# Self-attention of a decoder layer: exponentials become the stationary operand, sums come as a column, results are turned by TensorE, and the steps stand in a new order

## What is computed

```
q = einsum('ntc,hdc->nhtd', x, w_q); k = ...w_k; v = ...w_v
a = einsum('nhtd,nhsd->nhts', q, k) / sqrt(dk)
a = where(t < s, -inf, a);  a = softmax(a, axis=-1)
y = einsum('nhts,nhsd->nthd', a, v).reshape(n, t, h*d)
return y @ w_o
x = x + attn(layernorm(x), ...)
```

## Time and profile before

| | us |
|---|---|
| median of 3 runs | 2052.72 |
| lowest and highest run | 2051.78, 2059.14 |
| span of the profiled execution | 2060.4 |
| startup of self-attention (to the fourth NM), in the profile | 0 to 134 |
| self-attention, steady, in the profile | 134 to 852 |
| its last units | 852 to 894 |
| the rest of the layer | 894 to 2060 |

### The profile page before, as it was taken

The page is one execution under the profiler, slowest core; times in us unless marked ns, Lnnn a source line. Parts: engine busy times, 40 slices in busy tenths (PEclk is TensorE's granted clock), DMA queues, the critical chain, the costliest instruction groups (busy, mean ns, idle before and its releaser), DMA issues. The chain is left out here.

```text
span 2060.4 us, 40889 instructions
## 1 busy us (share of the span) xinstructions
PE 1842.1 (89%) x13992; PEld 972.5 (47%) x13992; DVE 1385.2 (67%) x3320; ACT 1291.6 (63%) x2477; POOL 1098.1 (53%) x1102
## 2 busy tenths in 40 slices
PE   4899999999999999979999999977899999588885
PEld 2456666666666666633333233322334443345553
DVE  5576666666666656457778777865798888554457
ACT  2677777777667776647777777773666666234442
POOL 2466666666566665633434433223667777455554
PEclk8899999999999999989999999997999999799998
DMA  6223232222322222313333113301011100233355
GB/s 187 69 64 71 61 71 59 66 63 63 73 63 60 65 67 55 74 44 63 62 63 61 29 37 63 57 14 33 21 30 67 50 22 22 85 92 114 93 191 193
DMA packets 102523, 141.00 MB, mean 68 GB/s; under 512 B 16400, under 2 KB 66352, under 8 KB 102320
## 3 DMA queue, kind: packets, MB, share of 16 engines
q1 hardware_dynamic: 95408, 119.44, 24.7%
q0 software_dynamic: 6912, 18.95, 2.5%
HBM read 53.77 MB, written 33.90 MB: 43 GB/s over the span
## 5 line engine op out<-in xcount | busy, mean ns | idle before, releaser
L771 POOL TENSOR_TENSOR a_P_lo<-a_PR,a_P_hi 128x384 f16<-128x384 f32 (+1 forms) x384 | 379.2, 999 | 336.7 <-ACT a_P_hi L580 252.4
L1333 DVE TENSOR_REDUCE x_NM<-x_pm 128x1 f32<-128x512 f32 x512 | 342.1, 687 | 97.8 <-PE x_pm L1069 95.2
L1254 ACT ACTIVATE x_PR<-x_pS 128x512 f32<-128x512 f32 x512 | 300.7, 601 | 111.8 <-PE x_pS L1085 105.8
L700 DVE CUSTOM_DVE_ANT_0 a_pm<-a_pm,a_causal 128x128 f32<-128x128 f32 (+3 forms) x512 | 251.9, 497 | 145.2 <-PE a_pm L463 136.1
L577 ACT ACTIVATE a_PR<-a_pS 128x384 f32<-128x384 f32 (+1 forms) x384 | 202.4, 527 | 100.6 <-PE a_pS L486 85.5
L580 ACT ACTIVATE a_P_hi<-a_pS 128x384 f16<-128x384 f32 (+1 forms) x384 | 202.1, 526 | 44.5 <-PE a_pa L500 44.5
L710 DVE TENSOR_TENSOR a_Y<-a_pa,a_RS 64x512 f32<-64x512 f32 x128 | 88.0, 688 | 137.5 <-ACT a_RS L593 135.5
L463 PE MATMUL a_pm<-a_KA,a_QA 128*128 128x128 f16 (+3 forms) x512 | 149.2, 303 | 29.0 <-DVE a_NM L700 21.0
L1097 PE MATMUL x_pa<-x_PR,x_V 128*32 128x256 f32 x2048 | 168.0, 401 | 1.7
L484 PE MATMUL a_pS<-a_QA,a_KA 128*128 128x512 f16 (+3 forms) x512 | 153.0, 301 | 11.4 <-DMA a_QB<-a_NMT 5.6
L500 PE MATMUL a_pa<-a_P_hi,a_V_hi 128*128 128x512 f16 (+3 forms) x512 | 152.6, 301 | 3.6 <-POOL a_P_lo L771 3.2
(11 more groups left out here) (411 smaller groups left out, 4994.7 us busy)
## 6 DMA issues: line engine op xcount, KB each, us to landing
a_QA<-a_nat_q_hi SPq DMA_DIRECT2D x128, 128.0 KB, 2.3
first_keys<-sent SPq DMA_DIRECT2D x80, 129.0 KB
a_QB<-a_nat_q_lo SPq DMA_DIRECT2D x64, 128.0 KB, 2.4
a_KA<-a_nat_k_hi SPq DMA_DIRECT2D x64, 128.0 KB, 2.4
a_KA<-a_nat_k_lo SPq DMA_DIRECT2D x64, 128.0 KB, 2.4
a_KB<-a_nat_k_hi SPq DMA_DIRECT2D x64, 128.0 KB, 2.4
e_ga<-back SPq DMA_DIRECT2D x16, 512.0 KB
first_keys<-in_w SPq DMA_DIRECT2D x12, 512.0 KB
```

The lines of the kernel that those rows point to most:

```text
L700: eng.tensor_tensor_reduce(out=pm[i % 2][:, 0:n], in0=pm[i % 2][:, 0:n], in1=causal[:, T - n:T], scale=1.0, scalar=NEG, op0=ALU.add, op1=A ...
L771: eng.tensor_tensor(P16[1][:, m % RH, 0:n], PR[:, m % RF, 0:n], P16[0][:, m % RH, 0:n], ALU.subtract).then_inc(s_el, 1)
L1254: eng.activation(PR[:, kc, j, :], pS[i % 2][:, :], ACT.Exp, scale=SCALE).then_inc(s_e, 1)
L1333: eng.tensor_reduce(NM[:, v % 2, c:c + 1], ring_bank("max", v, n)[:, :], AX.X, ALU.max, negate=True).then_inc(s_red, 1)
```

## The change

- AV (L549 to L551 now): for each pair of a key block and a block of 128 queries, the block of exponentials is the stationary operand and V moves: 65 columns for the terms with `V_hi` (64 of V and a column of ones), 64 for `V_lo`. Ten pairs a head and three terms: 120 matmuls a unit in place of 48. Queries now lie on partitions, and the sum of each row is a column beside its 64 values.
- ACT no longer runs LN and EX. DVE takes the reciprocals of four sums a head (L746) and multiplies four blocks of 64 columns (L748).
- POOL writes high and low parts to `Y16`. PE turns them, 8 transposes of 128 columns for each pair of heads (YT, L495), into `pp[1]` (from u = 32 on into `pp[0]`), and DVE copies the bank to `YT` (L758). QK 3 and V 1 wait for these copies, since they use the same bank.
- V: one ACT pass and one DVE pass of 512 columns a half (DVE took two of 256). The presets of ones and zeros shrink to one memset.
- WO comes one unit later (u - 6), and the last units have order numbers of their own.
- All order numbers are new, with a turn of 25 in place of 27. This moves steps on all engines, SP's DMAs among them.

```diff
-    V = [sb(f"V_{n}", [P, 2, TT, GH, P], F16) for n in ("hi", "lo")]
+    VW, OW = 72, 68
+    V_hi = sb("V_hi", [P, 2, TT, GH, VW], F16)
+    V_lo = sb("V_lo", [P, 2, TT, GH, D], F16)
...
-    RS = sb("RS", [P, 2, T], F32)
-    Y = sb("Y", [P, 2, T], F32)
-    YT = [sb(f"YT_{n}", [P, 2, F // P, T], F16) for n in ("hi", "lo")]
+    RC = sb("RC", [P, 2, TT], F32)
+    Y = sb("Y", [P, 2, TT, P], F32)
+    Y16 = [sb(f"Y_{n}", [P, 2, TT, P], F16) for n in ("hi", "lo")]
+    YT = sb("YT", [P, 2, F // P, 2, T], F16)
...
-    TURN = 27.0
-        ("SP", "CK"): (19.104,),
-        ("SP", "NP"): (45.09,),
+SELF_TURN = 25.0
+    ("SP", "CK"): (13.946,),
+    ("SP", "NP"): (39.099,),
...
+            if c == 3:
+                after(eng, s_yo, 2 * u - 4)
...
+            if h == 1:
+                after(eng, s_yo, 2 * u - 3)
...
+        def turn_values(u, q):
+            eng.wait_ge(s_yh, q + 1)
+            eng.wait_ge(s_yl, q + 1)
+            if u < NU:
+                eng.wait_ge(s_lo, 4 * u + 2 + 2 * (1 - q % 2))
+            elif q % 2 == 1 and u < NU + 2:
+                eng.wait_ge(s_xr, u - 5)
+            else:
+                eng.wait_ge(s_yo, q)
+            for z in range(2):
+                for t in range(TT):
+                    o = (z * TT + t) * P
+                    m = eng.transpose(turned_bank(u)[:, :].bitcast(F16)[:, o:o + P], Y16[z][:, q % 2, t, :], k.id16[:, :])
+            m.then_inc(s_yt, 1)
...
-                    for n, (v, p) in enumerate(((0, 0), (1, 0), (0, 1))):
-                        m = eng.matmul(pa[j % 2][:, P * kc:T], V[v][:, u % 2, kc, j, :], P16[p][:, i % RH, a:a + T - P * kc],
-                                       start=(kc == 0 and n == 0), stop=(kc == TT - 1 and n == 2))
+                    for t in range(kc, TT):
+                        o = a + (t - kc) * P
+                        hi, lo = (z[:, i % RH, o:o + P] for z in P16)
+                        out = pa[j % 2][:, t * OW:t * OW + D + 1]
+                        eng.matmul(out, hi, V_hi[:, u % 2, kc, j, 0:D + 1], start=(kc == 0 and t == 0), stop=False, skip_group_check=True)
+                        eng.matmul(out[:, 0:D], hi, V_lo[:, u % 2, kc, j, :], start=False, stop=False, skip_group_check=True)
+                        m = eng.matmul(out, lo, V_hi[:, u % 2, kc, j, 0:D + 1], start=False, stop=(kc == t), skip_group_check=True)
...
-                    eng.activation(RS[outs, pair, :], pa[j % 2][sums, :], ACT.Ln).then_inc(s_ln, 1)
-                eng.activation(RS[:, pair, :], RS[:, pair, :], ACT.Exp, scale=-1.0).then_inc(s_rc, 1)
...
-                eng.tensor_tensor(Y[outs, pair, :], pa[j % 2][outs, :], RS[outs, pair, :], ALU.mult).then_inc(s_y, 1)
+                o = values_of(j)
+                eng.reciprocal(RC[:, j % 2, :], o[:, :, D]).then_inc(s_rc, 1)
+                eng.wait_ge(s_rc, GH * u + j + 1)
+                eng.tensor_tensor(Y[:, pair, :, j % 2 * D:(j % 2 + 1) * D], o[:, :, 0:D],
+                                  RC[:, j % 2, :].unsqueeze(2).to_broadcast([P, TT, D]), ALU.mult).then_inc(s_y, 1)
...
+                eng.tensor_copy(YT[:, b % 2, 2 * g + pair, :, :].rearrange("p z t -> p (z t)"),
+                                turned_bank(v)[:, :].bitcast(F16)).then_inc(s_yo, 1)
```

More of the change, by code:

```diff
@@ L323, in self_attention @@
-    FIRST = {"ST": -16, "RS": -13, "XN": -11, "XH": -7.5, "XL": -6}
-    TURNED = {"PE": (-1.6, -1.0), "DVE": (-1.2, -0.5)}
-    def at(engine, step, u, i=0):
-        return u * TURN + PLACE[engine, step][i]
+    def at(engine, step, u, i=0):
+        if step == "WO" and u >= NU:
+            return NU * SELF_TURN + SELF_END[step][u - NU] + (1 if engine == "DVE" else 0.1 * i)
+        if step == "YT" and u >= NU:
+            return NU * SELF_TURN + SELF_END[step][2 * (u - NU) + i] + (1 if engine == "DVE" else 0)
+        return u * SELF_TURN + SELF_PLACE[engine, step][i]
@@ L442, in projections @@
                     transpose_x(b, h)
-            for c in range(4 if u < NU else 0):
+            if NU <= u < NU + 2:
+                yield from project_out(u)
+            for c in range(2 if u < NU else 0):
                 yield at("PE", "QK", u, c)
                 project_qk(u, c)
+            if 0 <= 2 * u - 5 < 2 * NU:
+                yield at("PE", "YT", u, 0)
+                turn_values(u, 2 * u - 5)
+            for c in range(2, 4 if u < NU else 0):
+                yield at("PE", "QK", u, c)
+                project_qk(u, c)
+            if 0 <= 2 * u - 4 < 2 * NU:
+                yield at("PE", "YT", u, 1)
+                turn_values(u, 2 * u - 4)
             for h in range(2 if u < NU else 0):
@@ L706, in scale_values, with turned_out @@
                 yield at("DVE", "Y", u, j)
-                eng.wait_ge(s_rc, q + 1)
+                eng.wait_ge(s_av, US * u + NS * (j + 1))
                 after(eng, s_yl, q - 1)
-                outs, _ = rows_of(j)
-                eng.tensor_tensor(Y[outs, pair, :], pa[j % 2][outs, :], RS[outs, pair, :], ALU.mult).then_inc(s_y, 1)
+                o = values_of(j)
[3 more added lines that the diff above has]
+                                  RC[:, j % 2, :].unsqueeze(2).to_broadcast([P, TT, D]), ALU.mult).then_inc(s_y, 1)
+        def turned_out(u):
+            b, g = u // NG, u % NG
+            for pair in range(2):
+                q, v = 2 * u + pair, u + 2 + pair
+                yield at("DVE", "YT", v, 1 - pair)
+                eng.wait_ge(s_yt, q + 1)
+                after(eng, s_wo, NG * (b - 1))
+                eng.tensor_copy(YT[:, b % 2, 2 * g + pair, :, :].rearrange("p z t -> p (z t)"),
+                                turned_bank(v)[:, :].bitcast(F16)).then_inc(s_yo, 1)
         def split_weights():
@@ L739, in next_stage @@
                                              in1=nat[0][1 - half][:, n, :], op0=ALU.max, op1=ALU.subtract).then_inc(s_pl, 1)
[L741 to L746 removed]
+        eng.memset(V_hi[:, :, :, :, D:D + 1].rearrange("p b t j o -> p (b t j) o"), 1.0).then_inc(s_pre, 1)
+        side_by_side(over(scale_values), over(turned_out), over(reduce_max), over(projections, NU + 6), over(norm, B), split_weights(), next_stage())
     def gpsimd_program(eng):
```

169 lines of the change are left out of this document (80 added, 89 removed).

## The result

| | us |
|---|---|
| changed kernel, median of 4 runs | 2075.17 (2072.1 to 2084.05) |
| kernel before beside it, median of 4 runs | 2054.36 (2051.78 to 2059.14) |
| ratio | 1.010 (95% interval 1.007 to 1.013) |
| forecast | 2085 (2046 to 2122), slower |

The change makes the kernel 1.0% slower. The forecast had the sign and the mechanism; two of its terms (the clock and the ends) were far off, in opposite directions. The profiled execution has a span of 2082.3 us, 21.9 above that of before (2060.4).

A forecast was written before the change was run, and what follows sets the result against it. PE was taken as the bound, busy 695.9 of 718 us in 28 units. Terms -61 + 73 - 21 + 10 + 13 + 18, and +1 at the ends, gave +33 on 2052.7: 2085 us, range 2046 to 2122.

The forecast's parts named there:

- the sign: Whole kernel: the change makes it slower, chance 0.66; within half a per cent 0.22, faster by more 0.12.
- the mechanism: Self-attention: a PE wait on the DMA chain behind the k projections, 2.6 us a unit, outweighs the 2.2 saved.
- the clock: Self-attention: PE waits bring half-clock stretches in two units of five, 1.6 us each, +18 us (0 to 46).
- the ends: Startup and last units: NP behind CK costs, replacing LN and EX saves; +1 us for both, within 4.
- AV and YT on PE: Self-attention, 28 units: AV falls from 6.56 to 3.5 us, YT adds 0.9; 2.2 us a unit less, -61 us.
- chain to S: From the last k projection: S starts at T + 6.65, PE has 4.1 us of work; 2.6 us wait, +73 us.
- late DMAs: CK issues on SP: a third of units has one about 1.2 us longer, +10 us (0 to 20).
- statistics: DVE, once in four units: 2.63 us less 0.8 to spare, PE waits 1.8 us longer seven times, +13 us.
- old waits: PE's earlier waits in the 28 units, some 22 us, all go as other engines catch up: -21 us.
- the rival that weight loads bound it: AV on PE: loads of 0.10 us don't overlap, AV costs 12 us a unit; about +200 us, 2290; chance 0.03.
- The case in which nearly every unit falls: Self-attention: clock falls in nearly every unit, +46 instead of +18, late DMAs +20: 2125 us; chance 0.14.
- PE stays the bound: Self-attention: chain done before PE arrives, 61 us and perhaps half the old waits saved: 1985 to 1995 us; chance 0.10.

The follow-up runs named there:

- the best version: Changed kernel with V's second half and AV's last two slots ahead of MX, values taken out early, WO between S's slots: ratio 0.972, 1974.8 against 2031.9 us.
- three such moves: Changed kernel, cumulatively: V and AV ahead of MX, values taken out early, WO between S's slots; 28 units 704.0, 688.5, 671.8 us.
- half the filler: Changed kernel with 4 added matmuls, in place of 8, whose result nobody reads, ahead of the first MX: ratio 1.000, 28 units 736.0 us.

## Why the prediction was right, and where it was off

Its sum for the 28 units was +32 us; measured are +43. For the ends and the rest it had +1; measured are -16 and -5. So it came out 11 us too high, well inside its range, but by errors that partly cancel: the clock was 26 us too low, the ends 17 too high. The mechanism was right; that the total is so close is in part luck.

| term | forecast | measured | from |
|---|---|---|---|
| AV and YT on PE | -61 | -58 | 30 AV matmuls from 586.30 to 587.20 are 0.030 us apart, 3.6 us a unit for 6.56; YT 587.20 to 587.65, twice |
| chain to S | +73 | +69 | the 61.5 + 11.6 us of waits ahead of MX and S (the shortest, under 0.15 us, counted in), plus 0.16 us a wait for the modelled end of the matmul ahead (9 us), less the next two |
| late DMAs | +10 | +10 | the other 22 units wait 2.08 us in the mean ahead of MX, the shortest 1.64 |
| statistics | +13 | +3 | in the six units in which a sequence comes in the wait is 2.64, not 2.08; two late issues are in it, see below |
| old waits | -21 | -18 | 3.9 us are left of 22.1 |
| clock | +18 | +44 | 27 stretches of 3.4 us at half, less one before: 26 x 1.7 |

The measured terms add up to +50, 7 more than the 43 there are. The stretches at half clock lie partly over the wait ahead of S (11.6 us in all), where they cost nothing and are counted here; that is up to 5.8 us.

**AV.** Right, against the rival that weight loads bound it: in the page, the first of the three lines of AV and its loads.

```profile
L549 PE MATMUL a_pa<-a_V_hi,a_P_hi 128*128 128x65 f16 x1280 | 147.9, 199 | 0.1
...
L549 PEld LDWEIGHTS a_pa<-a_V_hi,a_P_hi 128*128 128x128 f16 x1280 | 123.5, 101 | 15.4 <-issue 4.8
```

A load shows 0.101 us, and yet the starts are 0.030 apart, as in the earlier trace rows. The Trainium skill (TensorE: Matmul & The Clock Gate, "LDWEIGHTS (loading the stationary operand)") gives 107 ns for a load of 128 columns, near the 101 of this row. It states the length of a load, not the distance of two matmuls; taken for that distance, the figure does not hold here.

**The chain.** Right to 0.2 us at its issues and at S, from durations read in a kernel in which nobody waited for it; the landing of the last CK DMA, forecast at T + 5.9, came at T + 5.7 to 6.5 where the issues were on time and no statistics stood ahead. The two runs that reorder SP, one in each kernel, show that the place of the DMAs makes this wait; the landing 0.09 us ahead of each first MX ties it to CK.

**The statistics.** The step that failed is "less 0.8, PE waits 1.8 us longer". The statistics took 2.0 us there, not 2.63: the last of them showed 0.24 us where the earlier trace rows has 0.78. The low part of k started at T + 1.6 in place of T + 0.83, so 0.8 us late, and it was six times in the 28 units, not seven. The 0.56 us by which the wait is longer in these units is no clean measure: it holds two issues of 1.8 and 2.1 us, and PE itself comes to MX 0.6 us later there, since NM waits for maxima that stand behind the statistics on DVE. From T to the first MX, in units without a late issue, it is 6.8 us with statistics (three units) and 6.0 without (fifteen): 0.8 us, some 5 us in six units.

**Late DMAs.** The size was right, the reason in part. The earlier trace rows has seven issues of over 1.4 us, not eight; the next is 1.09. In the changed kernel seven of the 28 units have a CK issue of 1.2 us or more. In the 22 units of the table issues of 0.9 us and more make 6 us; most of the rest are five units in which the issues are on time and the fourth DMA lands 2.7 to 3.1 us after its issue instead of 2.3, which the forecast did not have.

**The clock.** The step that failed is "I take two units in five". It was drawn from two waits, 2.09 and 1.76 us long, of which one was followed by a stretch. In the changed kernel 26 of the 28 waits were, the shortest of 1.64 us; the two that weren't were 1.70 and 1.73 us long. The case in which nearly every unit falls had 0.14, and its price, +46, was right; it should have been the likeliest. The run with 8 added matmuls gives the price without any model: 40 us.

**The ends.** The step that failed is to let the saving on PE count only in the 28 units. The startup and the last units hold the other four: PE is busy 5.1 us less in the one (95.05 to 89.95) and 3.1 less in the other. The rest is waits that went: in the last units PE waited 4.8 us for POOL's low part of the output before, and 0.8 for DVE's copy of it now.

**The rest of the layer** is the same code, and its 5 us go with the time at half clock, which differs between any two profiles here: PE was busy at half clock for 94 us of it before and for 83 after, and half of that difference is 5.

**The rivals.** "PE stays the bound" had its point at 4.1 us of chain; the chain is 6.8. It describes the best version instead, where 5.8 us of work stand between T and the first MX (525.09 to 530.91 in one unit): that gives 0.972. "The loads don't overlap" is excluded by the starts 0.030 us apart.

## What to carry to other kernels

Count a new order from the moment an engine lets go of the last input to the moment it needs the result: conversions on two engines, every DMA issue on the queue, the landing; and against it only the work that stands between in the engine's own order. If the work is shorter, put there what is ready, but not so that several blocks with few banks come in a row, and look at what the moved step's own inputs wait for (here 57, then 16 and 17 us by three such moves). Here a wait of some two microseconds in every turn of the loop cost more than half as much again by the clock (73 us waited ahead of MX and S, and 40 to 44 lost at half clock); a queue's order has no value of its own, the same swap cost 1.6% under one order of PE and gave 1.9% under another.

## What the runs showed of the hardware

- Work that nobody needs can make a kernel faster: 48 us of added matmuls shortened the 28 units by 40 us, because the granted clock stayed at 1.00.
- Waits of 1.64 us and more were followed by 3.4 us at half clock in 26 of 28 units when they came once in 27 us. In the kernel before, one of 1.76 us was not followed, and with half the filler one of 2.15 us wasn't. I found no length that divides them.
- Matmuls of 64 or 65 columns, each with its own load of 128 x 128, keep 0.030 us from start to start over runs of 30 and more, though each load shows 0.101 us; at half clock 0.055 (593.11 to 593.66, eleven starts, 0.050 to 0.06).
- An issue on SP took up to 2.1 us where the median is 0.53 to 0.60; 11 of the 28 units have one of more than 1.2 us. The trace has a hint that the runs did not follow: a packet of the DMA queue that the profile calls "instruction" (q8) starts within 0.25 us of the start of each of these 11 issues, and of only 4 of the 306 that took under 0.7 us (124 to 850 us, the DMAs of the maxima left out). In the kernel before it is 17 of 18 late issues (of over 1.0 us) and none of 320. They come together; that the one makes the other, no run tried.
